# Swapping two ScalarE instructions in the K/V projection loop: the exponential of the keys ahead of the copy of the values

## What is computed

```python
q = elu(x @ Wq.T) + 1;  k = elu(x @ Wk.T) + 1;  v = x @ Wv.T
KV = einsum('bshd,bshe->bhde', k, v)            # summed over the sequence
out = einsum('bshd,bhde->bshe', q, KV) / (einsum('bshd,bhd->bsh', q, k.sum(1)) + 1e-6)
x = layernorm(x + out @ Wo.T)
x = layernorm(x + (silu(x @ wg.T) * (x @ wu.T)) @ wd.T)   # wg, wu, wd: int32 / 127
```

## Time and profile before

| | us |
|---|---|
| time, median of 2 runs | 1839.51 (1838.66 to 1840.35) |
| the profiled execution, its own time | 1836.44 |
| its span, slowest core (core 0) | 1834.9 |
| spans of all eight cores | 1822.0 to 1834.9 |

### The profile page before, as it was taken

The page is one execution under the profiler, slowest core; times in us unless marked ns, Lnnn a source line. Parts: engine busy times, 40 slices in busy tenths (PEclk is TensorE's granted clock), DMA queues, the critical chain, the costliest instruction groups (busy, mean ns, idle before and its releaser), DMA issues.

```text
span 1834.9 us, 23066 instructions; the slowest of 8 cores (1822.0 to 1834.9 us)
## 1 busy us (share of the span) xinstructions
PE 1557.7 (85%) x7424; PEld 684.0 (37%) x7424; DVE 520.3 (28%) x979; ACT 545.0 (30%) x801; POOL 42.1 (2%) x44
## 2 busy tenths in 40 slices
PE   2586755877999899988898888899899899989998
PEld 0232322323444344433343333344444344434443
DVE  1142342223311431232123333322321332133211
ACT  2432223111432252225123322522241234214213
POOL 0010001210000000000000000000000000000000
PEclk9898977988999999999899999999999999999999
DMA  8898347883345145424643331453255244512431
GB/s 234 262 321 254 97 140 193 308 282 116 104 144 151 49 111 166 122 75 138 200 139 69 87 121 47 106 172 114 75 138 152 73 115 133 154 41 71 147 100 46
DMA packets 213236, 255.28 MB, mean 139 GB/s; under 512 B 136320, under 2 KB 136320, under 8 KB 212096
## 3 DMA queue, kind: packets, MB, share of 16 engines
q1 hardware_dynamic: 213120, 253.81, 47.8%
HBM read 184.55 MB, written 37.75 MB: 121 GB/s over the span
## 4 chain that ended last, share of the span: by engine, by line
PE 68%; DMA 12%; DVE 7%; ACT 7%; issue 4%; SPq 1%; POOL 0%; DVEq 0%; ACTq 0%; POOLq 0%
PE ps_c L735 18%; PE ps_a L1135 16%; PE ps_b L1148 15%; PE ps_b L941 5%; PE ps_b L552 3%; PE ps_a L568 3%; DVE t L829 2%; DMA xT<-x_bf 2%; PE ps_a L552 2%; PE ps_b L568 2%; ACT texp L836 2%; DMA scr_wg<-wgu 2%; PE ps_a L816 2%; DVE q_fm L843 2%; DMA attnT<-wui 1%
## 5 line engine op out<-in xcount | busy, mean ns | idle before, releaser
L1135 PE MATMUL ps_a<-ln1T,wgu 128*128 128x512 bf16 x1536 | 367.2, 382 | 26.3 <-DMA ln1T<-ln_bf 9.4
L1148 PE MATMUL ps_b<-ln1T,wgu 128*128 128x512 bf16 x1536 | 368.4, 383 | 22.6 <-DVE h_fm L1175 22.5
L735 PE MATMUL ps_c<-wd_buf,h_fm 128*128 128x512 bf16 x1536 | 354.6, 391 | 0.0
L1167 ACT ACTIVATE silu_b<-ps_a,consts 128x512 bf16<-128x512 f32 x192 | 131.2, 687 | 522.6 <-PE ps_a L1135 464.7
L1175 DVE SCALAR_TENSOR_TENSOR h_fm<-ps_b,silu_b 128x512 bf16<-128x512 f32 x192 | 131.9, 690 | 488.6 <-PE ps_b L1148 453.4
L1135 PEld LDWEIGHTS ps_a<-ln1T,wgu 128*128 128x128 bf16 x1536 | 150.7, 99 | 213.2 <-issue 37.0
L1148 PEld LDWEIGHTS ps_b<-ln1T,wgu 128*128 128x128 bf16 x1536 | 150.5, 99 | 211.0 <-issue 36.0
L735 PEld LDWEIGHTS ps_c<-wd_buf,h_fm 128*128 128x128 bf16 x1536 | 153.3, 101 | 186.1 <-issue 19.8
L941 PE MATMUL ps_b<-wpair,attnT 128*128 128x512 bf16 x512 | 130.5, 413 | 31.0 <-DVE res L965 16.7
L816 PE MATMUL ps_a<-xT,wpair 128*128 128x512 bf16 x512 | 129.1, 403 | 31.4 <-DVE q_fm L843 26.8
L639 ACT ACTIVATE texp<-res 128x1024 bf16<-128x1024 f32 x64 | 67.3, 1051 | 293.3 <-DVE res L758 235.1
(11 more groups left out here) (61 smaller groups left out, 805.3 us busy)
## 6 DMA issues: line engine op xcount, KB each, us to landing
wgu<-scr_wg SPq DMA_DIRECT2D x168, 256.0 KB, 2.7
wgu<-scr_wu SPq DMA_DIRECT2D x168, 256.0 KB, 2.7
x_f<-x SPq DMA_DIRECT2D x56, 512.0 KB, 4.4
out<-outb SPq DMA_DIRECT2D x32, 512.0 KB, 2.7
outb<-wgi SPq DMA_DIRECT2D x14, 512.0 KB, 5.9
outb<-wui SPq DMA_DIRECT2D x14, 512.0 KB, 6.8
outb<-wdi SPq DMA_DIRECT2D x12, 512.0 KB, 6.7
wgu<-wdi SPq DMA_DIRECT2D x12, 512.0 KB, 8.0
```

The source lines that it names most:

```text
L735: t.matmul(d_view[:, pr, hl * 512:(hl + 1) * 512], h_fm[:, hm, sc * 128:(sc + 1) * 128], wd_buf[:, hm, hl * 512:(hl + 1) * 512], start=(hm ...
L1135: t.matmul(ps_a[:, (m % 2) * 512:(m % 2 + 1) * 512], wgu[:, 0, r, j * 128:(j + 1) * 128], ln1T[:, j, :], start=(j == 0), stop=(j == NJ - 1)),
L1148: t.matmul(ps_b[:, (m % 2) * 512:(m % 2 + 1) * 512], wgu[:, 1, r, j * 128:(j + 1) * 128], ln1T[:, j, :], start=(j == 0), stop=(j == NJ - 1)),
L1167: e.activation(silu_b[:, m % 2, :], ps_a[:, (m % 2) * 512:(m % 2 + 1) * 512], AF.Silu, scale=consts[:, 2:3]),
```

## The change

In each iteration `t_exp` is put ahead of `t_v` in the code, and so in ACT's list. Operands, shapes, waits and all other instructions stay.

```diff
                 bread(kbk, t_min)
                 tr_t1.end_write(t_min)
+                t_exp = P.op("scalar",
+                             lambda e: e.activation(texp[:], t1[:], AF.Exp),
+                             waits=[t_min, tr_texp.begin_write()])
+                tr_t1.add_reader(t_exp)
+                tr_texp.end_write(t_exp)
                 t_v = P.op("scalar",
                            lambda e, kr=kr, vps=vps:
                            e.activation(v_tm[:, kr, :, 0:HD],
...
                            waits=brd(vbk) + [tr_vtm[kr].begin_write()])
                 bread(vbk, t_v)
                 tr_vtm[kr].add_write(t_v)
-                t_exp = P.op("scalar",
-                             lambda e: e.activation(texp[:], t1[:], AF.Exp),
-                             waits=[t_min, tr_texp.begin_write()])
-                tr_t1.add_reader(t_exp)
-                tr_texp.end_write(t_exp)
                 t_k = P.op("vector",
```

## The result

The changed kernel takes 1949.56 us (median of 11 runs) against 1839.34 us for the kernel before: a ratio of 1.0595, 95% interval 1.0573 to 1.0618. It is slower by some 6%, 110 us. The forecast was 1951.5 us, in a range from 1927 to 1976.

What follows compares the result with a forecast made beforehand. PE, busy 85% of the span, was taken to bound the kernel. Waiting of 65.2 us (44.2 second sequence, 21.0 first) plus 46.8 us of clock gave 112.0 us on 1839.5: 1951.5 us, range 1927 to 1976.

Steps and rivals of the forecast that it cites:

- Steps 1 and 2: Loop of `phase1`: `t_v` and K(u+1) start 3.40 us later, V's 0.24 us hold goes; net 3.16 us per iteration.
- Step 3: First and last chunk lose nothing; K(2) to K(15) of the second sequence do: 14 gaps, 44.2 us.
- Step 4: First sequence: nothing lost up to K(3); K(4) to K(15) follow PE's own longer chain, 21.0 us without the clock.
- Step 5: DMAs queued behind the later cast of x should not bind, K(11) being tightest: priced at 0, 8 us at worst.
- Step 6: K bursts after the 4.40 us gap run partly at the 1.2 GHz level: 26 x 1.8 = 46.8 us.
- The held clock: Rival: the idle gap opens in the loop but the clock stays up, 1904.7 us; chance 0.07.
- The deeper fall: Rival: each gap in the loop costs the worst row's 2.76 us at the clock, 1976.5 us; chance 0.06.
- The hidden first half: Rival: DMA feed sets the first sequence's pace, so its 21.0 + 21.6 us vanish, 1908.9 us; chance 0.04.
- The other side: Rival: `t_min` done before V ends, so the exponential hides under V; 5 us gained, 1834.5 us; chance 0.03.

Runs made afterwards that it cites:

- the gap filled: Changed kernel plus 16 extra matmuls, results thrown away, in each of the 26 gaps ahead of K: 1901.82 us, ratio 1.0355 to the kernel before.
- The early minimum: Changed kernel, swap kept, with `t_min` issued ahead of the previous chunk's accumulation on DVE: 1831.13 us, ratio 0.9965 to the kernel before.
- the eight kernels with whole projections: All kernels run except the one with `t_min` early and K, V and their followers in two halves of 512 columns (ratio 0.9860 to the kernel before).

## Why the prediction was right

*Steps 1 and 2, the late copy.* Predicted: the copy 3.56 us after the small matmuls start, idle time 4.40, period without the clock 11.83. Measured: 3.57, 4.38, and 11.83 with the gap filled. The hold of V by `t_k` did vanish: K to V is 3.45 us (1095.22 to 1098.67). Both numbers came from reading the chain in one iteration to the hundredth of a microsecond and following the lists of the engines; nothing else was needed. The early minimum shows that the cause was this chain and not the order as such.

*Step 3, which gaps.* K(1) is not late (1.48 us idle, of which 1.37 were there before), K(2) to K(15) are. That K(1) kept its place was closer than the prediction knew. It put only an exponential of 1.06 us under V(0), but in the second sequence that exponential has a load of ACT's table of 1.28 us ahead of it:

```profile
993.62 1.28 ACT L590 ACT_TABLE_LOAD   x1 [5.70 <-DVE t L585]
```

In the kernel before it ran behind the copy (957.94 us); now it stands ahead of it, and the copy, which started 3.72 us after V(0) did, starts 3.83 us after it. The 0.11 us are the whole difference in K(1)'s idle time.

*Step 4, the first sequence.* Predicted 42.6 us with the clock, measured 42.4 in the traces of two different cores, and 40.5 to 45.4 core by core: that the two agree to 0.2 us is luck, that they agree to some 3 us is not. K(2) and K(3) of core 2 now wait for the copy by the profile, where core 0 of the kernel before waited for `xT`, but they start at 71.14 and 85.88 us instead of 71.10 and 85.81. Over all eight cores the small matmuls of chunk 2 start at 86.6 to 96.8 us before and at 87.2 to 96.4 after: nothing was lost up to there, as predicted.

*Step 5, the DMAs.* Priced at 0: K(11), the tightest, waits for the copy like all the others (at 194.16 us, predicted 195.8), and its 11.55 us wait for `xT` is absorbed. On cores 0 and 6 K(4) still waited for `xT`, 5.24 and 5.62 us instead of the 4.38 us of the copy; on the slowest core nothing of the kind shows.

*Step 6, the clock.* Predicted 1.8 us per gap, 46.8 in all. From the periods: 13.75 - 11.83 = 1.92 in the second sequence and 13.61 - 11.83 = 1.78 in the first, 48.2 us; from the runs with the filled gap 44, or 50 by the loops of all eight cores. The 1.8 was a choice between four rows from 1.60 to 2.76, and nothing in them singled it out: the row nearest in idle time (1.60) would have given 1946.3 us, still within the range. Of the total, the waiting was put a little too high (65.2 for 63 in the traces) and the clock a little too low (46.8 for 50), and the two errors cancel: the 2 us between forecast and median owe something to that. On this the Trainium skill, page TensorE: Matmul & The Clock Gate, was of two voices: its section HAM oscillation (a loop that waits in every pass pays in every pass) is what the chip did, while the advice under What's actually happening, that the ramp may be modelled at under 1% of the span, fails here: 0.0240 of the kernel's time.

*The rivals.* The held clock (1904.7) is what the kernel with filled gaps shows, 1901.8: the right price for a case that did not come about. The deeper fall came in one burst only near its size (K(2) of the second sequence, 6.29 us against 3.61). The hidden first half is refuted by the first sequence's loss of 40.5 to 45.4 us. The other side came true only where the minimum was moved: 1831.1 us, forecast for that case 1834.5. One sum of the prediction does not come out as written: 17 us for the clock's term below the forecast make 1934.5, not 1927; the lower end holds another 8 us that nothing accounts for, since the feed was priced at 0 to 8 us of loss. The measured time lies within the narrower range too.

Two smaller points were not as said. I expected K to wait for the copy in some 26 places; the profile has it 27 times and the two waits that it puts down to `t_k` besides. In those two the burst has 15 records instead of 16: the first one is missing, so that its start and its releaser are read off the second.

## What to carry to other kernels

On an engine that runs its list in order, put first what is ready first: an instruction inherits every wait of the one ahead of it, so ask of the new neighbour not how long it takes (1.06 us here) but what it waits for, on whatever engine that stands. If the time an idle gap adds to a loop is priced, add the clock: here the burst of matmuls behind it cost 1.7 to 1.9 us on top of 3.1 us of waiting per iteration of the second sequence. And before swapping two instructions, look one engine further up: moving the minimum gained what the swap lost, and 0.3 to 0.7% more.

## What the runs showed of the hardware

I had not expected that the price at the clock is nearly the same for an idle time of 2.5 us (8 extra matmuls, bursts of 5.2 to 5.3 us, 1944 us) and of 4.4 us (bursts of 5.2 to 6.3 us, 1950 us), and nothing at 1.7 us (1905 us) and 0.8 us (1902 us). Useless matmuls that shorten the idle time from 4.4 to 2.5 us bought 0.1% by the ratios (11 us, 0.6%, by the loops in the traces), four more of them 2.6% by the ratios of two chips and 2.0%, 37 us, by the loops.

For one burst it is a step: over all cores of the eight kernels with whole projections, a burst of K took either about 3.6 us or at least 4.9, and nothing between. For the idle time ahead of it there is no sharp edge. Counting the bursts of which all 16 records are there, none of 996 was slow after up to 1.8 us of idle time, 11 of 29 after 1.8 to 2.45 us, 166 of 188 after 2.45 to 2.6 us (nearly all of these with 8 extra matmuls), 35 of 43 after 2.6 to 4.0 us, and all 502 after more than that. So between 1.8 and 4.0 us the same gap can go either way, and only the two ends can be relied on in this kernel.
